# First attention of a two-layer transformer: the order of TensorE's work in a step's first slot, and a sixth expert added up tile by tile

## Chip, cores, metric

One core of one Trainium2 chip. The metric is the device time of one execution, in microseconds; the time of a kernel is the median of its runs. Engines are TensorE (PE; PEld is its weight load), VectorE (DVE), ScalarE (ACT), GpSimd (POOL) and SyncE (SP), which here only issues DMAs.

## What is computed

A batch of 16 sequences of 256 tokens with 128 channels, and a context of 64 tokens with 64 channels for each, go through two layers. The change touches the first attention and the mixture of experts at the very end; between them stand a gated feed-forward of layer 0 and a self- and a cross-attention block of layer 1.

```
x = x + attention0(layernorm(x), ctx)      # 16 heads of 8: causal self + cross, softmaxes apart, sum @ Wp + bp
x = x + ffn0(layernorm(x))
x = x + block1(layernorm(x), ctx)          # self- and cross-attention with their feed-forwards
idx = argmax(softmax(x @ gate_w.T + gate_b)); pos = place of a token in its expert; keep = pos < 640
hdn  = relu(buf[e] @ w1[e] + b1[e])        # 8 experts, 640 rows each, 128 -> 512
eout = hdn @ w2[e] + b2[e]                 # 512 -> 128
x = x + eout[idx, pos] * top_prob * keep
```

## The kernel before

Every engine runs a program of its own, and semaphores tie them together. An engine's instructions run in the order in which they are written; the order around the change is written out by hand.

**First attention (`l0_attention`).** The loop goes over 16 steps, one for each sequence (P = 128 tokens a tile, T = 256, U = 10 slots a step, G = 4 groups of heads). `tensor_slot`, `vector_slot`, `scalar_slot` and `gpsimd_slot` are called for each slot; a slot is counted as `s = 10 n + u`, and step n is the one whose scores run in it. Tables say what is done in which slot for which sequence:

- `tensor_scores(n, u)`: the transposed scores of two pairs of heads (L506, L510; cross heads L516 in slots 8 and 9). It waits for the exponential of the slot before (`exp_done`). In slot 0 it also waits for a small DMA on SyncE's queue (L857) that places the maxima among the rows of the query tile.
- `tensor_max(n, m)`: eight fills of the score banks for the maxima of the next sequence (`late` L544, `early` L553, both followed by the causal mask L523, and `cross` L562). Maxima 0 and 1 run in slots 8 and 9, 2 in slot 0, 3 in slot 1, 4 in slot 2, 5, 6 and 7 in slots 4, 5 and 6. All fill the same pair of PSUM banks (2 and 3), except for sequence 0, which alternates between two pairs; a fill waits until VectorE has reduced the one before (`max_done`). `vector_max` reduces the banks (L666, L661 for `cross`).
- `tensor_values`: probabilities times values (L578, L581; cross L589 in slot 1).
- `tensor_projection(use)`: everything that goes through the ring of two PSUM banks 6 and 7: layer norm turns, projections, turns of queries and keys, and the closing of a finished sequence. Slot 0 has two of these: `q0`, eight turns of the query tile of the sequence after next (L441), copied by ScalarE (L749); and `e4`, the closing product with Wp of the sequence before the previous one (L486), to which VectorE adds the bias (L718) and then the result to x (L722). A use waits until the use two places ahead in the ring is drained.

Within a slot TensorE runs scores, `late` and `early` maxima, values, ring uses, `cross` maxima. VectorE runs the same maxima first, then its ring drains, then `cross` maxima and layer norm pieces. `q0` exists for steps up to 13, `e4` from step 2 on, maximum 2 up to step 14.

**Experts (`experts`).** E = 8 experts, CT = 5 tiles of 128 rows each. In iteration n TensorE interleaves the four hidden groups of expert n (L2742), the turn of the tokens of expert n+1 (L2727) and the five output tiles of expert n-1 (L2767). The outputs of experts 0 to 5 go into banks 6 (four tiles) and 7 (one tile), with one signal `y_full` when all are there; VectorE adds the bias in two instructions (L2818, L2820), signals `y_out`, and then scales each tile and adds the tokens (`vector_gated`, L2810), with one `y_ready` a tile. Experts 6 and 7 have a bank and a signal for each tile (`vector_last_outputs`, L2832). In an iteration VectorE first handles the next expert's weights (L2794) and turn (L2789, L2790), then the outputs of the expert before, then `vector_gate`. GpSimd scatters each tile to the output with an indirect DMA (L2885) after its `y_ready`; a tile buffer `ys` is free again when the scatters of the expert two before are done (`stored`). SyncE loads weights and tokens of later experts, some of them after `y_out`.

Of the kernel before, what the change touches and what calls it, by code (L numbers as in the profile page):

```python
# [18 lines left out]
B, T, C, CC, TC = 16, 256, 128, 64, 64  # L19
# [3 lines left out]
K4 = HID // P  # L23
# [3 lines left out]
E = 8  # L27
CAP = 640
CT = CAP // P
# [256 lines left out]
def l0_attention(pr, mem, ffn, meanwhile):  # L286
# [4 lines left out]
    nc, io, psum = pr.nc, pr.io, pr.psum  # L291
# [76 lines left out]
    def batches(n, u, slots):  # L368

        pairs = [(part, *divmod(U * n + u - slot, U)) for part, slot in slots.items()]  # L370
        return [(part, batch) for part, batch, rest in pairs if rest == 0 and 0 <= batch < B]

    def projections(n, u):
        return batches(n, u, SLOT)
# [220 lines left out]
    def tensor_slot(s):  # L595
        n, u = divmod(s, U)
        if 0 <= n < B:
            tensor_scores(n, u)
        for m, batch in first_maxima(n, u):
            tensor_max(batch, m)  # L600
        if u in (3, 5, 7, 9) and 0 <= n < B:
            tensor_values(n, u // 2 - 1)
        if u == 1 and 0 <= n - 1 < B:
            tensor_values(n - 1, G)
        for use in projections(n, u):
            tensor_projection(use)
        for m, batch in last_maxima(n, u):
            tensor_max(batch, m)

# [253 lines left out]
    for slot in (tensor_slot, vector_slot, scalar_slot, gpsimd_slot):  # L863
        for s in range(U * FIRST, tail):
            slot(s)
# [1803 lines left out]
def experts(pr, mem, r):  # L2669
    nc, psum, tokens_in = pr.nc, pr.psum, pr.tokens_in  # L2670
# [12 lines left out]
    xT_full, xT_out, numbered = pr.sem("m_xT_full"), pr.sem("m_xT_out"), pr.sem("m_numbered")  # L2683
    h_full, h_out, y_full, y_out, y_ready = (pr.sem("m_" + x) for x in ("h_full", "h_out", "y_full", "y_out", "y_ready"))
    stored = [pr.sem(f"m_stored{i}") for i in range(2)]


    def sync_tokens(n):
# [5 lines left out]
    def sync_first_tokens():  # L2694

        z, rest = slice(0, C), slice(C, ROW)
        nc.sync.dma_start(xt[0][:, 0:3, z], by_tile(tokens_in, 0, 3)[:, :, z]).then_inc(half_there, 16)
        nc.sync.dma_start(xt[0][:, 3:CT, z], by_tile(tokens_in, 3 * P, 2)[:, :, z]).then_inc(tokens_there[0], 16)
        nc.sync.dma_start(xt[0][:, :, rest], by_tile(tokens_in, 0)[:, :, rest]).then_inc(rest_there, 16)

    def sync_experts():
        sync_first_tokens()
        sync_tokens(1)
        sync_tokens(2)
        for n in range(E):
            if n + 2 < E:
                if n:
                    nc.sync.wait_ge(h_out, 4 * n)
                r.sync_first(n + 2)
            if n + 1 < E:  # L2710
                if n:
                    nc.sync.wait_ge(y_out, n)
                r.sync_second(n + 1)
            if n + 3 < E:
                sync_tokens(n + 3)
# [29 lines left out]

    def out_of(n, t):

        if n >= E - 2:
            return psum[:, ((6, 7, 0, 1, 6), (2, 3, 4, 5, 0))[n - E + 2][t], 0:C]
        return psum[:, 6 + t // 4, (t % 4) * P:(t % 4) * P + P]  # L2750

    def signal_of(n, t):

        return n + 1 if n < E - 2 else E - 2 + CT * (n - E + 2) + t + 1

    def tensor_outputs(n, t):
        p, out = n % 2, out_of(n, t)
        if t == 0:
            if n and n < E - 1:
                nc.tensor.wait_ge(y_out, signal_of(n - 1, CT - 1))  # L2760
            nc.tensor.wait_ge(second_in, 32 * (n + 1))
            nc.tensor.wait_ge(h_out, 4 * (n + 1))
        if t == CT - 1 and n >= E - 2:

            nc.tensor.wait_ge(y_out, signal_of(E - 2, 0 if n == E - 2 else 2))
        for k in range(K4):
            inst = nc.tensor.matmul(out, hT[p][:, k, t * P:t * P + P], w2[p][:, k, :],  # L2767
                                    start=(k == 0 and (t % 4 == 0 or n >= E - 2)), stop=(k == K4 - 1),
                                    skip_group_check=True)
        if t == CT - 1 or n >= E - 2:  # L2770
            inst.then_inc(y_full, 1)

    def tensor_program():
# [49 lines left out]
        for t in range(CT):  # L2823
            vector_gated(n, t)

    def vector_last_outputs(n):
        p = n % 2
        nc.vector.wait_ge(gated, 2 * n + 2)
        nc.vector.wait_ge(stored[p], 80 * (n // 2))
        for t in range(CT):  # L2830
            nc.vector.wait_ge(y_full, signal_of(n, t))
            nc.vector.tensor_tensor(ys[p][:, t, :], out_of(n, t), b2[p][:, :], ALU.add).then_inc(y_out, 1)  # L2832
            nc.vector.wait_ge(y_out, signal_of(n, t))
            vector_gated(n, t)

    def vector_program():
        vector_weights(0)
        vector_turn(0)
        for n in range(E + 1):
            if n + 1 < E:  # L2840
                vector_weights(n + 1)
                vector_turn(n + 1)
            if n >= E - 1:
                vector_last_outputs(n - 1)
            elif n:
                vector_outputs(n - 1)
            if n < E:
                vector_gate(n)
# [173 lines left out]
```

## Time and profile before

| | us |
|---|---|
| median of 3 runs | 1374.11 (1371.72 to 1375.43) |
| the profiled execution | 1365.83 |
| its span, first to last instruction | 1364.1 |
| TensorE busy | 1268.4 (93%) |
| VectorE busy | 973.1 (71%) |
| ScalarE busy | 844.6 (62%) |
| GpSimd busy | 637.4 (47%) |
| mean granted TensorE clock | 0.976 of full speed |

The page has six parts; used here are the shares of the chain that ended last, and the answers of the trace: the chain in order of time, the timeline of one engine, and the busy time by window. A timeline row is start, duration, engine, line and operation, output and inputs, partitions x elements; behind it in brackets the idle time of the engine and what ended it. PEclk 1.00 is 2.4 GHz and 0.50 is 1.2 GHz.

### The profile page before, as it was taken

What the parts mean: (1) busy time and instruction counts of PE and PEld (TensorE: products, weight loads), DVE (VectorE), ACT (ScalarE), POOL (GpSimd) and SP (SyncE); (2) the same over time, 40 slices, a digit from 0 to 9 for tenths busy, and PEclk for the clock granted to TensorE, in tenths of its full rate; (3) what the DMA queues carried; (4) which work ended last, traced back from release to release, by engine and by line L of the source; (5) the groups of instructions that cost most, each with busy time, mean ns of one, the idle gap of its engine ahead of it and who ended that gap; (6) DMA issues with size and microseconds to landing.
All of it is one profiled execution on the core that took longest, in us unless ns stands there. A gap on an engine that the chain in (4) does not pass through costs nothing.

```text
span 1364.1 us, 43136 instructions
## 1 busy us (share of the span) xinstructions
PE 1268.4 (93%) x18030; PEld 827.8 (61%) x18030; DVE 973.1 (71%) x2243; ACT 844.6 (62%) x1305; POOL 637.4 (47%) x1087
## 2 busy tenths in 40 slices
PE   6999999998999999899999999989988999898895
PEld 4455555554455554456777777766766666676584
DVE  6788888875566555577888888866657887687243
ACT  3687787876666566657777777755545666542352
POOL 4456655543000102336667676544624654356265
PEclk7899999997999999999999999999989999999998
DMA  8000000000410000000001011012002222122461
GB/s 233 6 3 4 3 3 4 3 4 2 130 49 1 1 1 0 1 2 18 23 30 33 19 33 33 20 33 79 1 6 54 55 49 53 44 89 96 148 173 39
DMA packets 64096, 53.79 MB, mean 39 GB/s; under 512 B 10023, under 2 KB 58155, under 8 KB 63648
## 3 DMA queue, kind: packets, MB, share of 16 engines
q1 hardware_dynamic: 60000, 44.21, 11.7%
q0 software_dynamic: 2816, 6.11, 1.3%
q8 instruction: 144, 2.36, 0.8%
q10 hardware_dynamic: 1088, 0.72, 0.2%
q14 instruction: 48, 0.39, 0.1%
HBM read 20.35 MB, written 14.49 MB: 26 GB/s over the span
## 4 chain that ended last, share of the span: by engine, by line
PE 77%; DVE 12%; issue 4%; ACT 4%; POOL 1%; DMA 1%; SPq 0%; POOLq 0%; DVEq 0%; ACTq 0%
PE psum L1629 7%; DVE a_nm L666 5%; PE psum L1657 4%; PE psum L1289 4%; PE psum L1005 4%; PE psum L1007 4%; PE psum L1006 4%; PE psum L1251 3%; PE psum L2767 3%; PE psum L2117 2%; PE psum L1600 2%; PE psum L578 2%; PE psum L424 2%; PE psum L1641 2%; PE psum L2148 2%
## 5 line engine op out<-in xcount | busy, mean ns | idle before, releaser
L1712 DVE TENSOR_REDUCE b_nm<-psum 128x4 f16<-128x1024 f32 x128 | 156.5, 1223 | 52.3 <-PE psum L1634 51.6
L783 ACT ACTIVATE a_prob<-psum 128x768 f32<-128x768 f32 (+1 forms) x160 | 136.2, 853 | 51.1 <-PE psum L510 49.4
L835 POOL TENSOR_SCALAR_AFFINE_SELECT a_prob<-a_prob 128x512 f32<-128x512 f32 x128 | 84.7, 662 | 109.0 <-ACT a_prob L783 108.8
L666 DVE TENSOR_REDUCE a_nm<-psum 128x4 f16<-128x1024 f32 (+1 forms) x96 | 117.1, 1222 | 25.9 <-PE psum L523 24.8
L171 POOL TENSOR_TENSOR f_ln_rstd<-f_ln_tmp,pow_half 128x4 f32<-128x4 f32 x24 | 24.4, 1018 | 186.5 <-DVE f_ln_tmp L160 186.3
L1139 ACT ACTIVATE xo_sb<-psum,f_w_h_s 128x512 f32<-128x512 f32 x64 | 44.0, 688 | 82.7 <-PE psum L1007 82.6
L1629 PE MATMUL psum<-b_QTh,b_KTh 32*128 32x256 f16 x512 | 70.3, 272 | 7.2 <-DVE b_nm L1712 5.2
L1634 PE MATMUL psum<-b_KTh,b_QTh 32*128 32x256 f16 x512 | 70.6, 273 | 1.2 <-DVE b_nm L1712 1.2
L1634 PE MATMUL psum<-b_KTl,b_QTh 32*128 32x256 f16 x512 | 69.3, 268 | 0.0
L1634 PE MATMUL psum<-b_KTh,b_QTl 32*128 32x256 f16 x512 | 69.3, 268 | 0.0
L1629 PE MATMUL psum<-b_QTh,b_KTl 32*128 32x256 f16 x512 | 69.2, 268 | 0.0
L1629 PE MATMUL psum<-b_QTl,b_KTh 32*128 32x256 f16 x512 | 69.2, 267 | 0.0
L2885 POOL DMA_INDIRECT out_dram<-m_ys,m_number x40 | 42.1, 1053 | 43.1 <-DVE m_ys L2810 33.7
L1798 ACT ACTIVATE f_hT0h<-psum 128x1024 f32<-128x1024 f32 x32 | 32.8, 1024 | 45.2 <-PE psum L1641 45.2
L1835 POOL TENSOR_SCALAR_AFFINE_SELECT b_late<-f_hT0h 128x256 f32<-128x256 f32 x64 | 36.9, 600 | 37.0 <-ACT f_hT0h L1798 37.0
L1074 DVE TENSOR_TENSOR f_hlastl<-xo_sb,f_hlasth 128x512 f16<-128x512 f32 x32 | 22.1, 692 | 43.8 <-ACT f_hlasth L1140 43.8
L1074 DVE TENSOR_TENSOR f_hT1l<-xo_sb,f_hT1h 128x512 f16<-128x512 f32 x32 | 22.7, 709 | 40.8 <-ACT f_hT1h L1140 40.7
L1005 PE MATMUL psum<-f_hT0h,f_h_wh 128*128 128x512 f16 x128 | 48.6, 380 | 2.7 <-DVE f_hT0l L1068 2.6
L661 DVE TENSOR_REDUCE a_nm<-psum 128x8 f16<-128x512 f32 x64 | 41.1, 683 | 13.1 <-PE psum L562 13.1
L1641 PE MATMUL psum<-b_nmT,b_group_row 32*128 32x256 f16 x512 | 48.9, 268 | 0.0
L2225 DVE TENSOR_REDUCE c_nm<-psum 128x16 f16<-128x1024 f32 x32 | 37.7, 1219 | 15.3 <-PE psum L2135 15.3
L1005 PE MATMUL psum<-f_hT1h,f_h_wh 128*128 128x512 f16 x128 | 48.5, 379 | 0.0
(470 smaller groups left out, 4464.1 us busy)
## 6 DMA issues: line engine op xcount, KB each, us to landing
f_h_wh<-b_rden SPq DMA_DIRECT2D x64, 128.0 KB, 2.1
f_h_wh<-c_rden SPq DMA_DIRECT2D x128, 64.0 KB, 2.0
expert_in<-empty SPq DMA_DIRECT2D x8, 662.5 KB, 11.0
m_xt<-expert_in SPq DMA_DIRECT2D x7, 662.5 KB, 5.3
m_w<-in_L_ffn_w_dram SPq DMA_DIRECT2D x16, 256.0 KB
x_sb<-in_x_dram SPq DMA_DIRECT2D x8, 256.0 KB, 4.0
f_w_h_w<-in_L_ffn_h_w_dram SPq DMA_DIRECT2D x2, 1024.0 KB, 8.3
out_dram<-m_send SPq DMA_DIRECT2D x8, 256.0 KB, 2.4
```

The source lines that it names most:

```text
L666: nc.vector.tensor_reduce(out, psum[:, banks, :].rearrange("p i (a b) -> p i a b", a=groups), X, ALU.max, negate=True).then_inc(max_done, 1)
L783: nc.scalar.activation(prob[unit % 5][:, :, 0:width], psum[:, first:first + 2, 0:width], ACT.Exp, scale=SCALE).then_inc(exp_done, 1)
L835: nc.gpsimd.affine_select(out=diagonal, in_=diagonal, compare_op=ALU.is_ge, fill=0.0, base=0, pattern=[[0, 4], [1, P]], channel_multiplier ...
L1005: nc.tensor.matmul(bank, wh[:, k, m * P:m * P + P], xh[:, k, :], start=(k == 0), stop=False)
L1006: nc.tensor.matmul(bank, wh[:, k, m * P:m * P + P], xl[:, k, :], start=False, stop=False)
L1007: inst = nc.tensor.matmul(bank, wl[:, k, m * P:m * P + P], xh[:, k, :], start=False, stop=(k == K4 - 1))
L1289: inst = nc.tensor.matmul(bank[:, to], hT[n % 2][:, k, to], li3[:, k, :], start=(t == 0 and k == 0), stop=True, skip_group_check=True)
L1629: t.matmul(psum[:, first_bank + i, to], key[r, g, own], q[r, g, :], start=(k + first + second == 0), stop=False, skip_group_check=True)
L1634: inst = t.matmul(psum[:, 2 + i, to], q[r, g, own], key[r, g, :], start=(k + first + second == 0), stop=(first == 1), skip_group_check=True)
L1641: inst = t.matmul(psum[:, first_bank + i, k * T:k * T + T], self.group_row[r, g, :], self.nmT[n % 2][r, :], start=False, stop=True, skip_g ...
L1657: inst = t.matmul(self.pr.psum[D * j:D * j + D, 6, 0:T], self.group_col[:, g, :], self.prob[(unit + j // 2) % 4][:, j % 2, kb * T:kb * T + ...
L1712: v.tensor_reduce(self.nm[:, :, :].rearrange("p t (j r) -> p j t r", r=32)[:, 2 * e:2 * e + 2, :, g], self.pr.psum[:, 2:4, :].rearrange("p ...
```

## The change

In slot 0 of each step TensorE runs the ring uses right behind the scores, ahead of the fills of the maxima; in all other slots the order stays. VectorE's, ScalarE's and GpSimd's orders in the attention are as before.

In the experts a constant `TILED = 5` takes the place of `E - 2`: the sixth expert (n = 5) too gets a signal for each tile. Its tiles alternate between banks 6 and 7, so from the third tile on TensorE waits until VectorE has added the tile two before. VectorE adds and scales tiles 0 and 1 of the sixth expert ahead of the eighth expert's weights and turn, and tiles 2 to 4 behind them. The wait of SyncE is written with the new count and means the same event.

```diff
--- before.py
+++ after.py
@@ -596,14 +596,18 @@
         n, u = divmod(s, U)
         if 0 <= n < B:
             tensor_scores(n, u)
+        if u == 0:
+            for use in projections(n, u):
+                tensor_projection(use)
         for m, batch in first_maxima(n, u):
             tensor_max(batch, m)
         if u in (3, 5, 7, 9) and 0 <= n < B:
             tensor_values(n, u // 2 - 1)
         if u == 1 and 0 <= n - 1 < B:
             tensor_values(n - 1, G)
-        for use in projections(n, u):
-            tensor_projection(use)
+        if u:
+            for use in projections(n, u):
+                tensor_projection(use)
         for m, batch in last_maxima(n, u):
             tensor_max(batch, m)
 
@@ -2683,6 +2687,7 @@
     xT_full, xT_out, numbered = pr.sem("m_xT_full"), pr.sem("m_xT_out"), pr.sem("m_numbered")
     h_full, h_out, y_full, y_out, y_ready = (pr.sem("m_" + x) for x in ("h_full", "h_out", "y_full", "y_out", "y_ready"))
     stored = [pr.sem(f"m_stored{i}") for i in range(2)]
+    TILED = E - 3
 
 
     def sync_tokens(n):
@@ -2709,7 +2714,7 @@
                 r.sync_first(n + 2)
             if n + 1 < E:
                 if n:
-                    nc.sync.wait_ge(y_out, n)
+                    nc.sync.wait_ge(y_out, signal_of(n - 1, CT - 1))
                 r.sync_second(n + 1)
             if n + 3 < E:
                 sync_tokens(n + 3)
@@ -2745,13 +2750,13 @@
 
     def out_of(n, t):
 
-        if n >= E - 2:
-            return psum[:, ((6, 7, 0, 1, 6), (2, 3, 4, 5, 0))[n - E + 2][t], 0:C]
+        if n >= TILED:
+            return psum[:, ((6, 7, 6, 7, 6), (6, 7, 0, 1, 6), (2, 3, 4, 5, 0))[n - TILED][t], 0:C]
         return psum[:, 6 + t // 4, (t % 4) * P:(t % 4) * P + P]
 
     def signal_of(n, t):
 
-        return n + 1 if n < E - 2 else E - 2 + CT * (n - E + 2) + t + 1
+        return n + 1 if n < TILED else TILED + CT * (n - TILED) + t + 1
 
     def tensor_outputs(n, t):
         p, out = n % 2, out_of(n, t)
@@ -2760,14 +2765,16 @@
                 nc.tensor.wait_ge(y_out, signal_of(n - 1, CT - 1))
             nc.tensor.wait_ge(second_in, 32 * (n + 1))
             nc.tensor.wait_ge(h_out, 4 * (n + 1))
+        if n == TILED and t >= 2:
+            nc.tensor.wait_ge(y_out, signal_of(n, t - 2))
         if t == CT - 1 and n >= E - 2:
 
             nc.tensor.wait_ge(y_out, signal_of(E - 2, 0 if n == E - 2 else 2))
         for k in range(K4):
             inst = nc.tensor.matmul(out, hT[p][:, k, t * P:t * P + P], w2[p][:, k, :],
-                                    start=(k == 0 and (t % 4 == 0 or n >= E - 2)), stop=(k == K4 - 1),
+                                    start=(k == 0 and (t % 4 == 0 or n >= TILED)), stop=(k == K4 - 1),
                                     skip_group_check=True)
-        if t == CT - 1 or n >= E - 2:
+        if t == CT - 1 or n >= TILED:
             inst.then_inc(y_full, 1)
 
     def tensor_program():
@@ -2823,11 +2830,11 @@
         for t in range(CT):
             vector_gated(n, t)
 
-    def vector_last_outputs(n):
+    def vector_last_outputs(n, tiles):
         p = n % 2
         nc.vector.wait_ge(gated, 2 * n + 2)
         nc.vector.wait_ge(stored[p], 80 * (n // 2))
-        for t in range(CT):
+        for t in tiles:
             nc.vector.wait_ge(y_full, signal_of(n, t))
             nc.vector.tensor_tensor(ys[p][:, t, :], out_of(n, t), b2[p][:, :], ALU.add).then_inc(y_out, 1)
             nc.vector.wait_ge(y_out, signal_of(n, t))
@@ -2837,11 +2844,14 @@
         vector_weights(0)
         vector_turn(0)
         for n in range(E + 1):
+            before_turn = 2 if n == TILED + 1 else 0
+            if before_turn:
+                vector_last_outputs(n - 1, range(before_turn))
             if n + 1 < E:
                 vector_weights(n + 1)
                 vector_turn(n + 1)
-            if n >= E - 1:
-                vector_last_outputs(n - 1)
+            if n > TILED:
+                vector_last_outputs(n - 1, range(before_turn, CT))
             elif n:
                 vector_outputs(n - 1)
             if n < E:
```

## Rows read from the trace of the kernel before

**Rows 1.** Page, part 4: shares of the chain that ended last, by engine.

```profile
PE 77%; DVE 12%; issue 4%; ACT 4%; POOL 1%; DMA 1%; SPq 0%; POOLq 0%; DVEq 0%; ACTq 0%
```

**Rows 2.** Chain that ended last, in step 9: start us, us, what.

```profile
210.21 1.24 DVE a_nm L666
...
212.11 1.23 DVE a_nm L666
213.33 0.34 DVE a_res L718
...
213.70 0.34 DVE x_sb L722
...
214.04 1.23 DVE a_nm L666
...
215.32 0.40 PE psum L553 x8
```

**Rows 3.** Timeline, TensorE, slots 0, 1 of step 9 (in brackets: idle before).

```profile
211.00 0.23 PE L510 MATMUL psum<-a_QT,a_KT 32*128 32x128 f16 x2
211.49 0.39 PE L544 MATMUL psum<-a_KT,a_QT 32*128 32x256 f16 x4 [0.27 <-DVE a_nm L666]
...
211.98 0.62 PE L441 MATMUL psum<-ident,a_tok 128*128 128x128 f16 x8
...
213.04 0.28 PE L506 MATMUL psum<-a_QT,a_KT 32*128 32x256 f16 x2
...
213.39 0.39 PE L544 MATMUL psum<-a_KT,a_QT 32*128 32x256 f16 x4
```

**Rows 4.** Timeline, GpSimd, same stretch.

```profile
210.08 0.42 POOL L829 TENSOR_TENSOR a_tok<-a_qf,a_tok 128x128 f16<-128x128 f32 x1
```

**Rows 5.** Timeline, SyncE queue: the maxima's transfer, once in each step.

```profile
207.86 0.52 SPq L857 DMA_DIRECT2D a_QT<-a_nmT  x1
...
226.78 0.52 SPq L857 DMA_DIRECT2D a_QT<-a_nmT  x1
```

**Rows 6.** Busy time by window: us, PE busy (instructions), PEclk, DMA share, GB/s.

```profile
43.00:44.00 1.00, 0.47 (x10) 1.00 0.02 8
46.00:47.00 1.00, 0.97 (x20) 0.52 0.00 0
...
303.00:304.00 1.00, 0.71 (x20) 1.00 0.01 2
314.00:315.00 1.00, 0.77 (x16) 1.00 0.00 0
...
316.00:317.00 1.00, 0.72 (x20) 0.50 0.00 0
```

**Rows 7.** Timeline, TensorE, from slot 4 to slot 7: step 0, then step 2.

```profile
46.03 0.39 PE L506 MATMUL psum<-a_QT,a_KT 32*128 32x256 f16 x2
...
55.89 0.29 PE L457 MATMUL psum<-ident,a_nm 128*32 128x128 f16 x2
...
86.39 0.28 PE L506 MATMUL psum<-a_QT,a_KT 32*128 32x256 f16 x2
...
93.68 0.29 PE L457 MATMUL psum<-ident,a_nm 128*32 128x128 f16 x2
```

**Rows 8.** Timeline, GpSimd, scatters: fifth expert's last, sixth's first, the kernel's last.

```profile
1334.51 0.98 POOL L2885 DMA_INDIRECT out_dram<-m_ys,m_number  x1 [0.30 <-issue]
1337.48 1.06 POOL L2885 DMA_INDIRECT out_dram<-m_ys,m_number  x1 [1.99 <-DVE m_ys L2810]
...
1355.66 0.98 POOL L2885 DMA_INDIRECT out_dram<-m_ys,m_number  x1 [0.31 <-issue]
```

**Rows 9.** Timeline, VectorE and TensorE, around the sixth expert's last outputs.

```profile
1333.91 0.28 DVE L2790 TENSOR_TENSOR m_xTl<-psum,m_xTh 128x128 f16<-128x128 f32 x1
...
1336.27 0.35 DVE L2810 SCALAR_TENSOR_TENSOR m_ys<-m_ys,m_gate,m_xt 128x128 f32<-128x128 f32 x1
...
1334.25 1.05 PE L2767 MATMUL psum<-m_w,xo_sb 128*128 128x128 f32 x8
```

## Prediction

> **What bounds the kernel now.** I read the page first. The chain that ended last is 77% TensorE and 12% VectorE [rows 1], so an edit pays only where one of these two waits for the other on that chain. The change touches two places: slot 0 of each of the 16 steps of the first attention, and the last 30 us. For the first I read the chain inside one step in the middle, step 9, then the timelines of its engines. From the reduction at 210.21 to the reduction that ends at 215.27 the chain alternates between VectorE and TensorE: reduction of maximum 1, fill of maximum 2, reduction of 2, the two additions of the closing product (L718, L722), reduction of 3 at 214.04, and at 215.32 the fill of maximum 4 [rows 2]. All the `late` and `early` maxima share one pair of PSUM banks, so a fill cannot begin before the reduction ahead of it has ended. Behind 215.32 the chain is TensorE until the next step's maximum 1. Steps 2 to 13 repeat at one pace: the transfer of the maxima goes out at 207.86 and 226.78, 18.92 us apart [rows 5]. A delay inside the alternating stretch therefore has nothing to disappear into: it moves the whole step. For the end I read GpSimd: the scatters of experts six to eight, 15 of them, follow one another from 1337.48 to 1355.66 with 0.3 us between them, and 1.99 us of idleness stands ahead of the first [rows 8]. There GpSimd is the bound, and TensorE is not.
>
> **Part 1, slot 0.** Nothing is added or removed; eight query turns (L441) and four closing products (L486) go ahead of the fill of maximum 2. Today that fill starts at 211.49, after a wait for the reduction of maximum 1; turns and products start at 211.98, the scores of slot 1 at 213.04 [rows 3]. So 1.06 us of TensorE work moves ahead of the fill. Their operands are there: the token tile is written at 210.50 [rows 4], the closing product's operand a slot earlier, and they could start as soon as the scores' last products (L510, 211.00) are issued. How much of the wait they fill is bounded by 0.27 (the idle time in brackets) and 0.49 (from the start of L510 to the fill). I take 0.34, since the two short products need some 0.15. The fill of maximum 2 then starts 1.06 - 0.34 = 0.72 us later, at 212.2.
> What is behind it: reduction 2 starts 0.62 after its fill (211.49 to 212.11), so at 212.83 instead of 212.11. VectorE's own order is unchanged; the additions L718 and L722 stand behind reduction 2 in its queue and reduction 3 behind them, so that earlier products do not help: 1.23 + 0.34 + 0.34 and two gaps of 0.02 put reduction 3 at 214.76, against 214.04 [rows 2]. TensorE by now has scores at 212.7 and nothing else it may run: it waits for reduction 2 to end at 214.06 and fills maximum 3 at 214.1 instead of 213.39 [rows 3]. A wait of 0.27 has become one of about 1.05, and maximum 4 starts at 216.04 instead of 215.32. The exponentials of slot 1 and the copy of the turned query come slightly earlier, and nobody on the chain waits for them.
> Cost: 0.72 in each full step (bounds 0.57 and 0.79), and steps 2 to 13 are full: 12 x 0.72 = 8.6. Steps 0 and 1 have no closing product and step 14 no turn; each costs something between 0 and 0.72, and I take 0.35, the middle: 1.05. In the steps ahead of 0 no scores run and VectorE is behind anyway; in step 15 no maximum is left. Sum of the order alone: **+9.7**.
>
> **Part 1, the clock.** The wait of 1.05 falls into a stretch where TensorE's work is small. In this stage the granted clock fell twice after such stretches: in step 0, with the engine 0.47 busy at 43, from 2.4 to 1.2 GHz at 46, and at the end of step 14, with 0.77 at 314, to 1.2 GHz at 316; in step 14 at 303 the engine was 0.71 busy and the clock stayed [rows 6]. After the change slots 0 and 1 hold a wait of 1.05, longer than the gaps in step 0. The price is in the trace: from slot 4's scores to the turn of the maxima in slot 7 step 0 took 55.89 - 46.03 = 9.86 us at the low clock, step 2 with the same work 93.68 - 86.39 = 7.29 at the full one [rows 7], so 2.57 a fall. How many of 12 steps fall is not in the trace: bounds 0 and 12. One of the three stretches cited kept its clock, but a step that falls is longer and the next ones meet the chip at another moment. I take one step in three: 4 x 2.57 = **+10.3**.
> The Trainium skill ("TensorE: Matmul & The Clock Gate", "A second HAM failure mode: psum-queue depth-cycling") says that short idles between groups of matmuls, repeated with the cycling of PSUM banks, are enough to make the clock swing. The trace agrees in step 0. Its section "HAM oscillation — how this bites in real kernels" blames gaps of waiting for DMA, much longer than 1.05 us; by that rule no step falls and the sum keeps 9.7.
>
> **Part 2, the sixth expert.** Its outputs are added tile by tile. VectorE handles tiles 0 and 1 before the eighth expert's weights and turn, so their rows are ready before the turn's last instruction at 1333.91, where today the first one is ready at 1336.62 [rows 9]. GpSimd, done with the fifth expert at 1335.49, can go on at once: of 1.99 us idle 0.30 remain as issue time, **-1.7** [rows 8]. From there the scatters are back to back, and the last one starts at 1353.97. VectorE's extra instructions lie under that backlog of GpSimd. One wait is added on TensorE: the last tile goes into bank 6 and must wait until tile 2 is read, and VectorE reads tile 2 only after the turn, which ends at 1334.19, plus an addition of some 0.3; TensorE arrives at 1334.25 [rows 9]. This costs TensorE 0.3 us, with two of the eighth expert's four hidden groups and its outputs queued behind it. The eighth expert's rows come then about 1351, three us before GpSimd needs the last: hidden. Without that cover it would be +0.3.
>
> **Sum.** +9.7 + 10.3 - 1.7 = +18.3. The profiled execution took 1365.8 (span 1364.1), so its counterpart should take 1384.1. The median of the runs shown is 1374.1, 8.3 above the profiled one; I carry that difference over: **1392.4**.
>
> **Rivals.**
> *The order alone, no fall.* The 1.05 us wait is too short and the clock stays, as at 303. Then 1374.1 + 9.7 - 1.7 = **1382.1**; with one fall 1384.7. For it: the clock held through all of steps 2 to 13. Against it: the wait in these slots of step 9 is 0.27 today [rows 3], a quarter of what it becomes.
> *Faster: TensorE is what a step is made of, and VectorE absorbs the delay.* Filling the wait then gives 0.34 in each of the 12 full steps, -4.1, and the scatters -1.7: **1368.3**. It decides from the point where reduction 3 has 0.72 us to spare before maximum 4's fill. The rows show 0.05 (215.27 to 215.32) [rows 2], which speaks against it.
> *The order costs nothing.* The step regains the 0.72 in later slots, for instance where TensorE waits for a copy. Only the scatters count: **1372.4**. Against it: the chain behind 215.32 is TensorE almost alone.
> *The clock falls in half of the steps or more.* Seven falls are 18.0: **1400**. Against it: a fall lengthens the step and shifts the next.
>
> **How the numbers follow.** Forecast, with two to six falls: 0.50 (own range 1386 to 1397.5). Order alone: 0.32. Faster: 0.07. Costs nothing: 0.05. Many falls: 0.06. The range of 8 in 10 runs from 1380, where the order alone ends with its lower bound of 0.57 a step, to 1397.5, six falls. A change of 0.3%, 4.1 us, is about what a measurement tells from none: faster 0.07, within 0.05, slower 0.88.
>
> **What would show it.** Between two transfers of the maxima 19.6 us in a step without a fall and about 22.2 in one with; the fill of maximum 3 with 1 us idle before it by L666; no idle time before maximum 2's fill; stretches of PEclk 0.5 between steps 2 and 13, about four; an idle time of 0.3 instead of 1.99 before the sixth expert's first scatter; TensorE waiting some 0.3 for VectorE ahead of that expert's last tile. The prediction is wrong if the steps stay at 18.9, and wrong in its larger half if the clock holds.

## The result, and the profile after

The changed kernel takes 1397.4 us (median of 4 runs, 1395.62 to 1399.65) against 1374.77 for the kernel before in the same series of runs (each series runs on one chip): a ratio of 1.0176, 95% interval 1.0158 to 1.0194, so 22.6 us slower. A second measurement in another series gave 1.0157 (1.0128 to 1.0186). The forecast was 1392.4 and its range ended at 1397.5. Scaled to the 1374.1 us from which I had worked, the measured ratio gives 1398.3. Direction and mechanism held, and the size lies just above the range. One run of the kernel before in a later series fell into a slow state of the chip (2031.92 us at a granted clock of 0.55) and is left out of every comparison.

First the beat of the first attention. The transfer of the maxima leaves SyncE once in a step; its columns in the timeline are start us, us, engine, line, operation. Kernel after, three steps running:

```profile
205.45 0.52 SPq L861 DMA_DIRECT2D a_QT<-a_nmT  x1
...
225.28 0.52 SPq L861 DMA_DIRECT2D a_QT<-a_nmT  x1
...
246.35 0.52 SPq L861 DMA_DIRECT2D a_QT<-a_nmT  x1
```

The first spacing is 19.83 us and the second 21.07; before, it was 18.92 in every one of these steps [rows 5]. The short spacing shows the price of the order, the longer one the order and something else. TensorE's timeline in slots 0 and 1 of step 9, a step of the short kind (L544, L441, L486, L506 and L553 are the lines of rows 3; in brackets the idle time before):

```profile
208.58 0.23 PE L510 MATMUL psum<-a_QT,a_KT 32*128 32x128 f16 x2
208.74 0.62 PE L441 MATMUL psum<-ident,a_tok 128*128 128x128 f16 x8
209.20 0.66 PE L486 MATMUL psum<-a_wp,a_yT 128*128 128x128 f32 x4
209.79 0.39 PE L544 MATMUL psum<-a_KT,a_QT 32*128 32x256 f16 x4
...
210.40 0.22 PE L510 MATMUL psum<-a_QT,a_KT 32*128 32x128 f16 x2
211.69 0.39 PE L544 MATMUL psum<-a_KT,a_QT 32*128 32x256 f16 x4 [1.07 <-DVE a_nm L670]
...
213.82 0.40 PE L553 MATMUL psum<-a_KT,a_QT 32*128 32x128 f16 x8 [0.30 <-DVE a_nm L670]
```

As forecast, turns and closing product stand directly behind the scores, nothing waits ahead of maximum 2's fill (209.79), and TensorE waits 1.07 us ahead of maximum 3's (211.69), where rows 3 have 0.27 ahead of maximum 2's and nothing ahead of maximum 3's. Not forecast: 0.30 ahead of maximum 4's. The chain of waits shows whose it is (start us, us, what):

```profile
210.41 1.22 DVE a_nm L670
211.63 0.34 DVE a_res L722
211.97 0.02 issue
212.00 0.34 DVE x_sb L726
212.34 0.21 issue
212.55 1.22 DVE a_nm L670
```

In rows 2 reduction 3 follows the addition into x (L722 there, L726 here) with no gap. Here 0.21 us lie between them. The timelines of VectorE and GpSimd say more:

```profile
211.55 0.41 DVE L722 TENSOR_TENSOR a_res<-psum,a_bp 128x256 f32<-128x256 f32 x1
212.00 0.63 DVE L726 TENSOR_TENSOR x_sb<-x_sb,a_res 128x256 f32<-128x256 f32 x1
...
211.72 0.64 POOL L839 TENSOR_SCALAR_AFFINE_SELECT a_prob<-a_prob 128x512 f32<-128x512 f32 x1 [0.74 <-ACT a_prob L787]
```

The addition takes 0.63 us. In the kernel before it took 0.42 to 0.43 in all 16 steps. It now runs while GpSimd's select is still going on. In the kernel before that select had ended 0.55 us ahead of the addition (213.70, rows 2), as its row of GpSimd shows:

```profile
212.51 0.64 POOL L835 TENSOR_SCALAR_AFFINE_SELECT a_prob<-a_prob 128x512 f32<-128x512 f32 x1 [2.01 <-ACT a_prob L783]
```

The second sum is the clock. Busy time by windows of the kernel after (us, PE busy, PEld, DVE, ACT, POOL, granted clock as a share of 2.4 GHz, DMA share, GB/s), in the step before one of the long spacings, and then the whole stretch from 60 to 300 us:

```profile
127.00:128.00 1.00, 1.00 (x19) 0.46 (x18) 0.14 (x1) 1.00 (x2) 0.44 (x1) 1.00 0.00 0
128.00:129.00 1.00, 0.07 (x4) 0.00 (x0) 1.00 (x1) 1.00 (x3) 0.43 (x2) 1.00 0.00 0
129.00:130.00 1.00, 0.86 (x16) 0.43 (x20) 0.96 (x3) 0.59 (x2) 0.64 (x1) 0.76 0.00 0
130.00:131.00 1.00, 1.00 (x16) 0.39 (x8) 1.00 (x2) 0.00 (x0) 0.00 (x0) 0.50 0.06 16
131.00:132.00 1.00, 1.00 (x20) 0.36 (x12) 0.73 (x3) 0.00 (x0) 0.00 (x0) 0.50 0.00 0
...
60.00:300.00 240.00, 221.62 (x3514) 130.04 (x3514) 191.84 (x394) 173.15 (x258) 129.84 (x234) 0.94 0.01 3
```

TensorE is 0.07 busy from 128 to 129 (the wait of 1.07 us), and from 129.5 the clock is 1.2 GHz for 3.4 us. For the same 240 us the kernel before has 1.00. There are eight such stretches from step 2 to step 13, mostly of 3.4 us, one of 6.8. The wait of 1.07 stands in all twelve of these steps, those without a fall too.

Third, the experts. GpSimd's scatters of the kernel after, around the sixth expert's first (1364.59), and one of ScalarE's rows behind them:

```profile
1363.30 0.98 POOL L2895 DMA_INDIRECT out_dram<-m_ys,m_number  x1 [0.30 <-issue]
1364.59 0.98 POOL L2895 DMA_INDIRECT out_dram<-m_ys,m_number  x1 [0.30 <-issue]
...
1375.32 0.98 POOL L2895 DMA_INDIRECT out_dram<-m_ys,m_number  x1 [4.59 <-DVE m_ys L2817]
...
1370.66 0.80 ACT L2876 ACTIVATE u_sb<-psum,m_b 128x640 f32<-128x640 f32 x1 [4.90 <-remote]
```

The 1.99 us of idle time ahead of the sixth expert's first scatter [rows 8] have become 0.30: part 2 does what it says. But a wait of 4.59 follows that the kernel before did not have in its profile, and behind it stands a ScalarE that starts 4.90 us late. The last experiment weighs whether that is the change's.

### The profile page after: what moved, and what is told of

It reads as the page before. It is cut to its first block, busy times and chain, and to the rows that moved or that the text cites. A ratio compares the mean times of both kernels' runs of the same rounds, so it can differ in the third digit from the quotient of the medians.

```text
span 1397.9 us, 43139 instructions
## 1 busy us (share of the span) xinstructions
PE 1285.2 (92%) x18030; PEld 835.0 (60%) x18030; DVE 978.6 (70%) x2246; ACT 843.4 (60%) x1305; POOL 635.2 (45%) x1087
## 4 chain that ended last, share of the span: by engine, by line
PE 77%; DVE 11%; issue 5%; ACT 3%; DMA 1%; POOL 1%; SPq 1%; POOLq 0%; DVEq 0%; ACTq 0%
PE psum L1633 6%; PE psum L1661 4%; PE psum L1293 4%; PE psum L1009 4%; PE psum L1011 4%; PE psum L1010 4%; PE psum L1255 3%; DVE a_nm L670 3%; PE psum L578 2%; PE psum L2774 2%; PE psum L424 2%; PE psum L1604 2%; PE psum L2121 2%; PE psum L1645 2%; PE psum L2152 2%
## 5 line engine op out<-in xcount | busy, mean ns | idle before, releaser
L1010 PE MATMUL psum<-f_hT0l,f_h_wh 128*128 128x512 f16 x128 | 48.5, 379 | 0.0
```

Source lines behind the costliest of these rows:

```text
L1010: nc.tensor.matmul(bank, wh[:, k, m * P:m * P + P], xl[:, k, :], start=False, stop=False)
```

## The experiments

Fourteen profiles are compared, the two given ones and twelve more. A step's length is the spacing of the maxima's turns on TensorE; the kernel before has 18.91 in steps 2 to 12.

**The kernel before once more.** For the scatter of the method.

> The kernel before, profiled once more. Three theories are at stake. (A) The order in slot 0 costs 0.92 us in a step without a fall of the clock (19.83 against 18.91 between two turns of the maxima) plus falls, and the tile edit gains 1.7. (B) The tile edit is what delayed the experts by 10.2 us in the profile of after, where ScalarE and VectorE started up to 5 us after the matmuls they waited for. (C) Such delays in the experts belong to both kernels and to chance; the profiled execution of before, 8.3 us below its median, simply had none. Under A and C this profile is near 1372 to 1376 and shows delays of 2 to 5 us in the experts; under B it shows none there and takes about 1366.

Measured 1.0004 (0.9988 to 1.0021), 1365.99 us, steps of 18.92 (one of them 18.91), no fall of the clock between 60 and 300 us. So 0.3% can be told from nothing. Its profile reached the first step at 37.2 us and the given one at 35.1: executions of one kernel differ by some 2 us in the start-up alone, which is to be remembered where single profiles are subtracted. About 1366 us and no delay in the experts is what was written down for (B), that the tile edit delays them. That it doesn't is shown by the tiles alone, below.

**The order alone.** The experts are those of the kernel before.

```diff
+        if u == 0:
+            for use in projections(n, u):
+                tensor_projection(use)
         for m, batch in first_maxima(n, u):
...
-        for use in projections(n, u):
-            tensor_projection(use)
+        if u:
+            for use in projections(n, u):
+                tensor_projection(use)
```

> Only slot 0's order is changed; the experts are those of before. A: +22.8 us against before as in the profile of after (about 1397), steps of 19.8 us without a fall, and seven or eight falls of the clock between steps 1 and 14. If only the wait counted and the falls were chance: +12 (1386). B: the experts show no delay here and this kernel is about 8 us below the kernel after (1389). C: delays in the experts in some executions here too, and 1 to 2 us above the kernel after (1399), by the 1.7 of the tiles.

Measured 1.0152 (1.0120 to 1.0184), +21.1 us: nearly all of the loss, and no delay in the experts. Turn by turn against the kernel before, in us:

| steps | order alone | before | difference |
|---|---|---|---|
| 0 and 1 | 22.22, 19.09 | 20.82, 18.88 | +1.6 |
| 2 to 12 without a fall (4) | 19.83 | 18.91 | +0.92 each |
| 2 to 12 with a fall (7) | 20.60 to 21.06 | 18.91 | +1.7 to +2.15 each |
| 13 (with a fall), 14 | 19.98, 19.87 | 18.10, 19.80 | +1.95 |
| sum | | | +21.0 |

The order costs 0.92 in each of 12 steps, 11.0. The eight falls cost 8.3, on average 1.04 each and 0.8 to 1.25 singly (step 13 is counted against the 19.02 that it takes with the clock held up, below); steps 0, 1 and 14 cost 1.7.

**The tiles alone.** The order is that of the kernel before, the sixth expert's outputs go by tile.

> Only the sixth expert's outputs are handled by tile; slot 0 is as before. A and C: 1.7 us below before (1373), the idle time ahead of the sixth expert's first scatter 0.3 instead of 1.99 us, and a wait of TensorE of about 0.3 ahead of that expert's last tile. B: 8 us above before (1383), with a wait of several us of TensorE for the last weights, since these are only loaded after the sixth expert's last addition.

Measured 0.9989 (0.9974 to 1.0005), -2.0 us by the medians of 12 and 22 runs, which by itself is not distinguished from no change. The trace shows the gain where it was forecast. GpSimd, fifth expert's last scatter, sixth's first, the kernel's last:

```profile
1331.67 0.98 POOL L2891 DMA_INDIRECT out_dram<-m_ys,m_number  x1 [0.30 <-issue]
1332.96 0.98 POOL L2891 DMA_INDIRECT out_dram<-m_ys,m_number  x1 [0.31 <-DVE m_ys L2813]
...
1350.99 0.98 POOL L2891 DMA_INDIRECT out_dram<-m_ys,m_number  x1 [0.30 <-issue]
```

From the fifth's last to the kernel's last 19.32 us, where rows 8 give 21.15: 1.83 less. TensorE's forecast wait of 0.3 ahead of the last tile (1331.61) is not there, its row has no bracket. With the tile edit in and the order of before, experts one to four take 8.6 to 8.7 us each and nothing is late: (B) is out.

**The new order with the clock held up.** In slot 1, where TensorE waits 1.07 us, it computes four products of 128x512 whose result nobody reads. The `wait_ge` ahead of them sees to it that the PSUM bank into which they go is free.

```diff
         if u == 0:
             for use in projections(n, u):
                 tensor_projection(use)
+        if u == 1 and 1 <= n < B - 1:
+            nc.tensor.wait_ge(ys_ready, 3 * (n - 1) + 1)
+            tensor_warm(pr, 4, 4)
```

> Slot 0's order changed, and in slot 1 of steps 1 to 14, where TensorE waits for the reduction of maximum 2, four products of 128x512 into a PSUM bank that the cross values overwrite; nobody reads them. They fit into the wait (4 x 0.22 = 0.86 of 1.05 us). If the falls of the clock come from this wait, they are gone: every step 2 to 12 takes 19.8 us and the kernel is about 12 us above before (1386), 10 below order alone. Rival: the falls have another cause, or the products delay the fills; then falls remain or steps are longer than 20, and the time is that of order alone (1397) or above.

Measured 1.0084 (1.0052 to 1.0115), +12.0 us. TensorE's timeline in the same slot (the row of the products has three of the four):

```profile
201.20 0.81 PE L87 MATMUL psum<-hide_later,identb 128*128 128x512 bf16 x3 [0.16 <-issue]
202.11 0.39 PE L544 MATMUL psum<-a_KT,a_QT 32*128 32x256 f16 x4
...
60.00:300.00 240.00, 231.56 (x3712) 135.59 (x3716) 195.07 (x404) 181.57 (x269) 133.47 (x240) 1.00 0.01 3
```

The last line is its window from 60 to 300 us: clock 1.00, against 0.94 after. The eleven steps are 19.83, each of them. More work in the wait makes the kernel 9.1 us faster than the order alone: filling that wait takes the falls away, and they are 9 us of the loss. The products themselves cost nothing: the steps are as long as those of the order without a fall. Whether as much unread work at another place of the step would do the same wasn't run.

**The whole change once more**, in a series in which the kernel before takes 1375.98.

> The kernel after, profiled once more. On the chip where order alone cost 21.1 us and the tiles gained 2.0, the sum is 19.1, a ratio of 1.014 to before. If the delays of the experts in the first profile of after belong to that execution or chip (C), this profile shows the seven falls and steps of 19.83 to 21.1 us again, and no stall of several us in the experts. If they come from the two edits together (B), TensorE again waits for the last weights by some 5 us and the ratio is 1.018 or more.

Measured 1.0157, +21.6 us; 19.83 without a fall, seven falls from step 3 to step 13, one of them of 6.8 us (step of 22.81). The experts are late again (9.5 to 9.7 us each, one wait of 6.8 of ScalarE), so the delays are not those of one execution, against the sign written down for (C). TensorE does not wait 5 us for weights either, the sign of (B): its longest wait there is 4.26, for ScalarE.

**The query turns alone ahead of the maxima**; the closing product stays behind.

> Of slot 0 only the eight query turns go ahead of the fill of maximum 2; the closing product stays behind it. Theory: the turns take 0.46 of TensorE and fill 0.34 of its wait, so a step costs 0.12 (19.03 instead of 18.91), the wait ahead of maximum 3 is about 0.2 to 0.5, too short for the clock to fall; 1.5 us in all, ratio 1.001. If moved work costs in proportion, it would be 0.46/1.06 of 0.92, 0.40 a step and 5 us, with a third or so of the falls; ratio 1.005 to 1.008.

Measured 1.0027 (1.0011 to 1.0042), steps of 19.12, +0.21, where 0.12 was expected and 0.40 by the rival. No fall between 60 and 300 us, though the wait ahead of maximum 3 is 0.43 now.

**The addition into x moved behind reduction 3**, on top of the order with the clock held up.

```diff
+        if u == 1 and 0 <= n - 2 <= B - 3:
+            vector_added(n - 2)
```

Here `vector_added` holds the wait and the addition that stood at the end of `vector_epilogue`.

> Order changed and products in the wait as in order_warm; in addition VectorE adds a sequence's result to x (0.43 us alone, 0.63 in slot 0 of the changed order, where it overlaps GpSimd's select of 0.64) behind the reduction of maximum 3 instead of ahead of it. If the 0.20 us by which a step without falls exceeds the predicted 0.72 is that addition running beside GpSimd's select, the steps come down from 19.83 to about 19.6 and the addition takes 0.43 again or no longer counts; 3 us below order_warm. If the 0.20 has another cause, steps stay at 19.8.

Measured 1.0131 (1.0103 to 1.0160), +17.9 us, steps of 19.93 instead of the expected 19.6: a miss. Some 3.6 of the 17.9 lie in step 14 alone (23.37 against 19.80), where the clock is low twice, for 10.2 and 13.7 us. VectorE and TensorE of this kernel:

```profile
203.45 0.41 DVE L725 TENSOR_TENSOR a_res<-psum,a_bp 128x256 f32<-128x256 f32 x1
204.20 1.23 DVE L673 TENSOR_REDUCE a_nm<-psum 128x4 f16<-128x1024 f32 x1 [0.34 <-PE psum L523]
205.34 0.42 DVE L733 TENSOR_TENSOR x_sb<-x_sb,a_res 128x256 f32<-128x256 f32 x1
205.68 0.60 DVE L188 TENSOR_SCALAR a_z<-x_sb,aln_mv,aln_rstd 128x128 f32<-128x128 f32 x2
...
206.42 0.41 PE L418 MATMUL psum<-ident,a_z 128*128 128x128 f32 x2 [0.32 <-DVE a_z L188]
```

The addition is back at 0.42 us, and reduction 3 starts 1.89 behind reduction 2 instead of 2.14. But the normalisation (L188) has slipped behind it with the addition, and TensorE waits 0.32 for that instead. The gain moved to the next wait. It doesn't refute the collision, and doesn't show it either.

**The select moved instead of the addition.** The select of slot 1 waits until the addition is done; its result is read several slots later.

```diff
         nc.gpsimd.wait_ge(exp_done, unit + 1)
+        if u == 1 and n >= 2:
+            nc.gpsimd.wait_ge(x_done, n - 1)
```

> The new order with the four unread products, and in each step from the third on the select of GpSimd that runs beside the addition into x waits until that addition is done. The selects are read only several slots later, so nobody waits for them. Theory (the two engines hinder each other): the addition is back at 0.43 us, the third reduction starts 0.20 earlier, and a step without a fall takes 19.63 instead of 19.83 us; over 12 steps 2.4 us, so 9.6 above the kernel before instead of 12.0. Rival (the addition takes 0.63 for another reason, or what follows waits for something else): the step stays at 19.83 and the kernel 12.0 above.

```profile
201.09 0.41 DVE L725 TENSOR_TENSOR a_res<-psum,a_bp 128x256 f32<-128x256 f32 x1
201.53 0.43 DVE L729 TENSOR_TENSOR x_sb<-x_sb,a_res 128x256 f32<-128x256 f32 x1
201.88 1.22 DVE L673 TENSOR_REDUCE a_nm<-psum 128x4 f16<-128x1024 f32 x1
```

0.43 again, and every step from 2 to 12 takes 19.62 or 19.63 instead of 19.83: as the collision has it, the rival is out. In this profile the end of the first attention lies 10.4 us behind that of the kernel before, against 13.4 with the collision. The times do not show it: 1.0099 (1.0077 to 1.0121), that is +10.5 to +16.5 us, with the expected 9.6 below the interval, from 4 runs that spread from 1373.42 (the profiled one) to 1382.03, wider than the 2.4 us at stake. So the collision is shown in the step, and its worth in the whole time is not.

**The closing product alone ahead of the maxima.**

> Only the closing product ahead of the maxima in a step's first slot; the query turns stay behind, the experts are those of the kernel before. Theory (the halves add up): a step without a fall takes 0.92 - 0.21 = 0.71 us more than 18.91, so 19.6; TensorE still waits 0.8 us or more before the third maxima fill, so about eight falls of the clock come with it, some 1.1 us each; 8.5 + 9 = 17 us above the kernel before. Rival (it is only both together that starve TensorE): steps of 19.1 to 19.3 with no fall, 3 to 5 us.

Measured 1.0034 (1.0017 to 1.0051), steps of 19.22, no fall: near the rival, and my theory was wrong in both numbers. TensorE waits 0.52 here ahead of maximum 3's fill:

```profile
197.09 0.39 PE L544 MATMUL psum<-a_KT,a_QT 32*128 32x256 f16 x4 [0.52 <-DVE a_nm L671]
...
197.40 0.42 DVE L727 TENSOR_TENSOR x_sb<-x_sb,a_res 128x256 f32<-128x256 f32 x1
```

The addition is short, so the collision needs both halves. Alone they cost 0.21 and 0.31, together 0.92: 0.20 are the collision, and 0.20 more appear only with both. That fits a wait of 0.27 ahead of maximum 2's fill which each half alone can use up and both together only once (0.46 and 0.60 us of work cost 0.21 and 0.31); no run tests it.

**Tiles, and unread products at the two falls of the kernel before**, in step 0 and step 14.

> A try at a version better than both: the tile edit alone, and products that nobody reads in the waits of TensorE in slots 1 and 2 of step 0 and slots 5 and 6 of step 14, ahead of the falls of the clock at 46 and 316 in the profile of before. If these falls come from these waits, the two stretches stay at 2.4 GHz: 2.6 us less for step 0 where it fell, up to 3 for steps 14 and 15, and 2.0 for the tiles; ratio 0.995. Rival: step 15 is paced by ScalarE's exponentials, the clock does not matter there, and only the tiles count, 0.999.

Measured 0.9989 (0.9973 to 1.0005), the rival's figure and not the 0.995 of the theory: no more than the tiles alone. The fall at 46 us is gone, as it was in the profile of the tiles alone without any help, and the clock fell at 304.6 and 325.1 for 6.8 and 10.2 us, where the kernel before has one stretch of 13.7 from 315.7 in the profile given and two of 6.8 and 10.2 in its two others. So the products did not help in step 14. The tile edit comes out fastest in both of its forms, 0.1% under the kernel before, but neither is distinguished from no change.

**The late select in the new order, nothing unread.**

> The new order whole, without unread products, with only the late select of the last series: the addition into x is short again, and TensorE waits about 0.87 us before the third maxima fill where the new order has 1.07 and either half of it alone at most about 0.5. Theory (the falls belong to the length of that wait, and 0.87 lies nearer to 1.07): a step without a fall takes 19.63 us and about eight of the twelve still have one at 0.8 to 1.25 us, so 9.6 + 9 = 18.5 us above the kernel before. Rival (the falls need the whole 1.07): no fall between 60 and 300 us, and 7.5 to 9.6 us above.

Measured 1.0140 (1.0114 to 1.0165), +20.6 by the medians. Steps without a fall 19.63, eight with one at 20.6 to 21.0 and step 13 with one at 19.95, clock 0.94 from 60 to 300 us. One expectation was wrong: the wait ahead of maximum 3's fill is not 0.87 but still 1.07, since the late select shortens what comes behind reduction 2 and not what comes ahead.

```profile
208.42 0.39 PE L544 MATMUL psum<-a_KT,a_QT 32*128 32x256 f16 x4 [1.07 <-DVE a_nm L670]
```

So the falls come at 1.07 and not at 0.52 or 0.43. In between the profiles have one more value, which comes once in each: in step 1, where nothing was closed yet, the wait at this place is 0.98 in five of them, and no fall follows in any. Kernel after:

```profile
66.98 0.39 PE L544 MATMUL psum<-a_KT,a_QT 32*128 32x256 f16 x4 [0.98 <-DVE a_nm L670]
```

**The kernel before a third time**, for where a slower chip loses its time.

> The kernel before, unchanged, for where a slower chip loses its time. Theory: if this chip's runs of it lie near 1375 us, the attention and the stages up to the start of the experts take what they take in the profile read for the prediction, within 3 us, and the stretch from the routing's last product (1264.7) to the end takes about 109 us instead of 99.4, with ScalarE and VectorE starting 2 to 5 us late in the last experts. If they lie near 1366 us, that stretch takes 99 to 100. Rival: a slow chip loses its time over all stages.

Measured 1.0013 (0.9992 to 1.0034). This series' runs of it lay at 1365.6 and the stretch from the routing's last product to the end took 99.4, so only the half of the expectation that speaks of 1366 us was put to the test. The other half rests on all profiles together. From that product to the end, in us:

| the kernel before takes in that series | kernel | routing's last product to the end |
|---|---|---|
| 1366 | before (three profiles) | 99.4, 99.8, 99.4 |
| 1366 | order alone, with clock held, with late select; closing product alone | 99.3, 99.4, 99.3, 99.6 |
| 1366 | tiles alone | 96.8 |
| 1374 to 1376 | after (two profiles), tiles with unread products | 106.8, 107.5, 109.8 |
| 1374 to 1376 | experts of the kernel before: query turns alone; addition moved; late select | 109.1, 109.2, 106.3 |

Three kernels with untouched experts lose 7 to 10 us there in the series of 1374 to 1376, "slower" from here on. The number of the chip alone doesn't decide it: the kernel before took 1365.6 in one series on a chip numbered 15 and 1373.9 in another. Their rows show the same signs as those of the kernel after. GpSimd's first scatter of an expert, first in the order alone (series at 1366), then in the query turns alone (series at 1376):

```profile
1332.43 1.06 POOL L2889 DMA_INDIRECT out_dram<-m_ys,m_number  x1 [1.99 <-DVE m_ys L2814]
...
1341.09 1.06 POOL L2889 DMA_INDIRECT out_dram<-m_ys,m_number  x1 [1.99 <-DVE m_ys L2814]
```

```profile
1337.85 1.06 POOL L2890 DMA_INDIRECT out_dram<-m_ys,m_number  x1 [3.03 <-DVE m_ys L2815]
...
1347.42 1.06 POOL L2890 DMA_INDIRECT out_dram<-m_ys,m_number  x1 [3.06 <-DVE m_ys L2815]
...
1365.82 0.98 POOL L2890 DMA_INDIRECT out_dram<-m_ys,m_number  x1 [4.37 <-DVE m_ys L2815]
```

An expert takes 9.57 us instead of 8.66, and near the end there is a wait of 4.37 where the kernel after has 4.59. So these waits come without the change. No profile of the kernel before itself was taken in a slower series; that its 8 to 10 us lie there is inferred from kernels which share its experts.

## Why the prediction was right and wrong

| term, us | forecast | measured |
|---|---|---|
| order, steps 2 to 13 | 8.6 | 11.0 |
| order, steps 0, 1 and 14 | 1.05 | 1.7 |
| clock | 10.3 | 8.3 (order alone); 10.0 and 9.1 (the two profiles of the whole change) |
| sixth expert | -1.7 | -2.0 |
| sum | 18.3 | 19.1 by the parts; 22.6 and 21.6 for the whole |

A fall is what its step takes above 19.83, in step 13 above 19.02.

**Order, 0.72 a step: the term was right for what it counted and left one thing out.** With the collision taken away, a step takes 19.63 - 18.91 = 0.72 us more, exactly the sum. With it, 0.92. The step that failed is the term 1.23 + 0.34 + 0.34 behind "VectorE's own order is unchanged". The order was unchanged, but I took the durations of rows 2 over as they stood, and did not ask what GpSimd does at the moment to which the addition moves. The addition came to lie beside a select that in the kernel before had ended 0.55 us ahead of it. The Trainium skill has it ("GPSIMD Engine Reference", section "1. Specifications"): GpSimd's interfaces to SBUF are shared with VectorE, with contention for VectorE instructions that have two SBUF inputs. The trace agrees: the addition into x, with two inputs in SBUF, goes from 0.42 to 0.63; the addition a_res ahead of it, with one in PSUM, overlaps the same select and stays at 0.41. Over 12 steps the term was 2.4 us too small: 11.0 instead of 8.6.

**Steps 0, 1 and 14**: 1.7 in the order alone, 1.05 forecast. It is not a fixed price: step 0 took 22.22 there, and 20.82, as in the kernel before, in the second measurement of the whole change, whose step 1 took 19.52 instead of 19.09.

**The clock: mechanism right, both factors wrong, the product near by luck.** I had 4 falls at 2.57 = 10.3. There are eight at 1.04 = 8.3 in the order alone, and the kernel with the unread products is 9.1 faster. The price failed because rows 7 come from a low stretch of 6.8 us (46.0 to 52.8) in a step with no wait above 0.53 ahead of them. For that stretch the 2.57 was right: step 0 of the tiles alone had no fall and took 18.25, against 20.82. Here most stretches last 3.4 us. The one step of the kernel after with 6.8 took 22.74, which is 2.91 above 19.83, near the 2.57. The count failed because of the sentence that a longer step "meets the chip at another moment": falls did skip steps (the table has four without), but more than half were hit. I had also read the fall in step 14 wrongly. The rows that I showed end at 315 and go on at 316; between them TensorE stood still, for longer than anywhere in steps 2 to 13, and the clock fell inside that second (kernel before, window row and TensorE's timeline):

```profile
315.00:316.00 1.00, 0.00 (x0) 0.84 0.00 0
...
316.23 0.45 PE L562 MATMUL psum<-a_KcT,a_QT 32*128 32x64 f16 x10 [1.46 <-DVE a_nm L666]
```

So one of the two falls that I cited followed a single wait of 1.46, and not a busy share of 0.77: a better precedent for a wait of 1.05 than the one I gave.

The rule of the Trainium skill that I had weighed ("TensorE: Matmul & The Clock Gate", "A second HAM failure mode: psum-queue depth-cycling") agrees with the runs; the one in "HAM oscillation — how this bites in real kernels", by which no step would fall, does not, the waits here being 1.07 us and not for DMA.

**The sixth expert: right**, 1.83 instead of 1.69 in the scatters. The forecast wait of TensorE did not come. It was costed at nothing, and nothing it cost.

**The rivals.** "The order alone, no fall" (1382.1) would have needed falls not to happen; the kernel with held clock shows what it would have been, 12.0 minus 2.0 for the tiles = 10.0 above. "Faster" and "costs nothing" fell with the step of 19.83. "Falls in half of the steps or more" (1400, chance 0.06) was about right in its count (seven, where seven or eight came) and 8 to 10 us over in its price (18.0 for 8.3 to 10.0); that it is nearest to the measured time is luck. The range had no row that made a seventh fall unlikely, but the falls did not carry the time out of it: its upper end allowed them 15.4 us and they cost 8.3 to 10.0. What did is the order, 2.4 and 0.65 too small, and the rest that follows.

**The rest, which is the larger part of the miss.** Order alone +21.1 and tiles -2.0 make +19.1; both measurements of the whole change gave more, 21.6 and 22.6. The intervals of the parts, each about 4 us wide or more, allow that, and the two were taken in slower series, in which the order alone was not run. These 2.5 to 3.5 us are not attributed. Between the turns of the first and the last step the whole change takes 22.8 and 20.9 us more than the kernel before in its two profiles, the order alone 21.0: in the first 1.8 us are found there, most of it in the low stretch of 6.8 us, and in the second nothing is. So of the 4.3 us by which the forecast fell short, the terms in the table explain 0.8, because 3.0 too little for the order and 2.3 too much for the clock and the tiles nearly cancel, and the cause of the rest stays open. Comparing the two given profiles gives 33.8 us instead, and would mislead: 3.0 of them lie ahead of the first step and 7.4 behind the routing's last product, where the profile after shows the waits of a slower series and the one before, at 1365.8, does not. That I carried the 8.3 us between profile and median over to the forecast was right: forecast and measured ratio are both against the median.

## What to carry to other kernels

When work is moved ahead of a wait, write down not only who starts later, but what every other engine is doing at the moment to which each instruction moves: a VectorE instruction with two inputs in SBUF that comes to lie beside a GpSimd instruction can cost half as much again (0.63 for 0.42 us here). When an alternation between two engines gains a wait of about 1 us in every round, ask what the clock does, and price a fall by the length of the low stretch. And if such a wait can't be removed, filling it with unread products can be worth more than it costs: here 9 us of 21.

## What the runs showed of the hardware

- With a wait of 1.07 us in each step of about 20 us the granted clock went to 1.2 GHz in seven to nine of twelve steps; with waits of 0.52 or 0.43 at that place, and with the 0.98 of step 1, it did not. Low stretches of 3.4 us cost 0.8 to 1.25 us, those of 6.8 cost 2.6 in step 0 and 2.9 and 3.0 in steps 2 and 3; why the short ones cost less than half isn't shown.
- The same waits do not always bring a fall. In step 0 of the kernel before, three waits of 0.33, 0.47 and 0.53 us, the last of them ending at 43.84, stood ahead of the fall at 46.0; with the tiles alone step 0 has the same three waits, and the clock stayed at 2.4 GHz.
- Four unread products of 128x512 in that wait kept the clock at 2.4 GHz from 60 to 300 us and cost nothing: steps of 19.83 with and without them.
- Beside a select of GpSimd the addition of two tiles in SBUF took 0.63 us instead of 0.42. By the rows the two overlap by 0.36 us (GpSimd's spans are rough) and the delay is 0.20.
- One kernel, unchanged, takes 1365.6 us in one series and 1376.0 in another. What the profiles show of it lies in the expert stage, where an expert takes 9.3 to 9.7 us instead of 8.7, and in one to three waits of 2 to 5 us of GpSimd near the end. Its cause stays open.
